# Top-8 expert selection in the router: eight rounds of maximum, index and knock-out in place of the MAX8 and FIND_INDEX8 instructions

## The reference

```python
router_logits = x @ gate_weight.T
router_probs = softmax(router_logits, axis=-1)                # 32 experts
router_top_value, router_indices = top_k(router_probs, 8)
routing_weights = router_top_value / clip(sum(router_top_value), 1e-12)
prim = router_indices[:, :4]; sec = router_indices[:, 4:]
sim_cand = sim[sec[:, :, None], prim[:, None, :]]
best_sim = max(sim_cand, -1); best_primary = prim at argmax(sim_cand, -1)
new_sec = where(best_sim < 0.5, sec, best_primary)
combine = sum(one_hot([prim, new_sec], 32) * routing_weights[..., None], 1)
for each expert e: y = y + (silu(x @ wg) * (x @ wu)) @ wd.T * combine[:, e]
```

## Time and profile before

| what | value |
|---|---|
| three timed runs | 7908.31, 8304.48 and 8369.88 us; median 8304.48 us |
| the profiled execution, whole | 7862.98 us |
| its span on the slowest core (core 0) | 7861.4 us |
| span of the other seven cores | 7813.4 to 7840.3 us |
| TensorE busy in matmuls | 5358.2 us, 68% of the span |
| VectorE busy | 2143.0 us, 27%, in 3227 instructions |
| ScalarE busy | 959.6 us, 12% |

### The profile page before, as it was taken

How to read it: one execution, slowest core, us unless ns; L and a number is a source line. 1 busy time by engine, 2 the same in 40 slices (tenths; PEclk the granted TensorE clock), 3 DMA queues, 4 the chain that set the end, 5 groups by cost and what they waited for, 6 DMA issues and landing times.

```text
span 7861.4 us, 58171 instructions; the slowest of 8 cores (7813.4 to 7861.4 us)
## 1 busy us (share of the span) xinstructions
PE 5358.2 (68%) x20631; PEld 2173.4 (28%) x21044; DVE 2143.0 (27%) x3227; ACT 959.6 (12%) x1288; POOL 34.6 (0%) x69
## 2 busy tenths in 40 slices
PE   3444665104777777777777787777777777777777
PEld 0111122001333333333333332333333333333332
DVE  5444544553222212121212121212122221212121
ACT  1103320000111010101010101010111101010101
POOL 0000000000000000000000000000000000000000
PEclk7766678556988888888888888888888888888888
DMA  4111001001332332333332323333323333333323
GB/s 163 38 48 59 1 23 58 9 0 58 101 103 98 106 98 104 97 108 99 106 100 104 96 103 97 104 101 102 103 100 100 100 104 99 105 94 106 100 107 123
DMA packets 146027, 692.91 MB, mean 88 GB/s; under 512 B 17136, under 2 KB 17264, under 8 KB 91696
## 3 DMA queue, kind: packets, MB, share of 16 engines
q1 hardware_dynamic: 136448, 646.94, 24.8%
q0 software_dynamic: 9296, 42.21, 1.6%
HBM read 680.70 MB, written 8.39 MB: 88 GB/s over the span
## 4 chain that ended last, share of the span: by engine, by line
PE 47%; DMA 21%; DVE 14%; issue 9%; ACT 8%; DVEq 1%; ACTq 0%; SPq 0%; POOL 0%; POOLq 0%
PE P L1162 37%; DMA arena_f<-wd 20%; ACT arena_b L1192 5%; DVE arena_b L1153 3%; DVE arena_f L1179 3%; PE P L1206 2%; PE P L678 2%; PE P L889 2%; PE P L828 1%; PE P L844 1%; ACT arena_b L783 1%; DVEq L158 1%; ACT arena_b L812 1%; PE P L507 1%; DMA arena_f<-wg 0%
## 5 line engine op out<-in xcount | busy, mean ns | idle before, releaser
L1162 PE MATMUL P<-arena_b 128*128 128x512 bf16 x12042 | 3042.9, 416 | 787.0 <-DVE arena_b L1153 767.9
L1162 PEld LDWEIGHTS P<-arena_b 128*128 128x128 bf16 x12288 | 1278.0, 105 | 2552.3 <-issue 1367.1
L1206 PE MATMUL P<-arena_b 128*128 128x512 bf16 x6020 | 1562.4, 419 | 583.5 <-ACT arena_b L1192 514.9
L1206 PEld LDWEIGHTS P<-arena_b 128*128 128x128 bf16 x6144 | 632.6, 106 | 1510.8 <-issue 965.4
L1214 DVE TENSOR_TENSOR arena_f<-arena_f,P 128x1024 f32<-128x1024 f32 x256 | 312.6, 1221 | 1808.1 <-PE P L1206 1808.1
L1153 DVE CAST arena_b<-arena_f 128x2048 bf16<-128x2048 f32 x384 | 469.7, 1223 | 1071.1 <-DMA arena_f<-wg 1071.1
L1179 DVE TENSOR_TENSOR arena_f<-arena_f,P 128x1024 f32<-128x1024 f32 x192 | 234.5, 1221 | 1857.2 <-PE P L1162 1857.2
L1192 ACT CAST arena_b<-arena_f 128x768 bf16<-128x768 f32 x512 | 425.5, 831 | 1704.9 <-DMA arena_f<-wd 1704.9
L1176 ACT ACTIVATE arena_f<-P 128x1024 f32<-128x1024 f32 x192 | 196.5, 1023 | 3372.5 <-PE P L1162 3353.2
L678 PE MATMUL P<-arena_b 128*128 128x512 bf16 x502 | 142.7, 450 | 196.4 <-DVE arena_b L671 195.6
L1182 DVE TENSOR_TENSOR arena_b<-arena_f 128x1024 bf16<-128x1024 f32 x192 | 235.3, 1225 | 20.0
(11 more groups left out here) (185 smaller groups left out, 1528.5 us busy)
## 6 DMA issues: line engine op xcount, KB each, us to landing
arena_f<-wg SPq DMA_DIRECT2D x384, 1024.0 KB, 4.9
arena_f<-wd SPq DMA_DIRECT2D x512, 384.0 KB, 3.1
arena_f<-x_win POOLq DMA_DIRECT2D x32, 768.0 KB, 5.1
arena_f<-wq SPq DMA_DIRECT2D x16, 1024.0 KB, 5.9
arena_f<-wo SPq DMA_DIRECT2D x16, 1024.0 KB, 6.0
arena_f<-x_win POOLq DMA_DIRECT2D x16, 512.0 KB, 14.5
out<-arena_f POOLq DMA_DIRECT2D x16, 512.0 KB, 3.5
arena_f<-wkv SPq DMA_DIRECT2D x4, 1024.0 KB, 5.5
```

What stands on the lines that cost most here:

```text
L1162: mk.op("pe", lambda E, ps=ps, par=par, c=c, s2=s2: E.matmul(out=ps[:, s2 * 512:(s2 + 1) * 512], lhsT=wbf2[par][:, c * 128:(c + 1) * 128], ...
L1206: first=(ei == 0 and j == 0): E.matmul(out=ps[:, s2 * 512:(s2 + 1) * 512], lhsT=wdbf[par][:, (ei * NDJ + j) * 128:(ei * NDJ + j + 1) * 128 ...
```

## The change

The three instructions of the top 8 (L1017, L1018, L1020) go, and with them the tensor `rIdx`. In their place VectorE copies the 32 probabilities to a scratch row and makes eight rounds. Round k takes the maximum of the row, compares the row with it, turns the comparison into 0 where it holds and 1,000,000 where not, adds the row 0..31, and takes the minimum, which is the first place of the maximum. The one-hot row `rH[k]`, which before was made after the weights, is now made in the round; in the first seven rounds three further operations set the chosen place of the scratch row to -1. The weights are computed after the rounds. `rws` has 320 columns in place of 512. Nothing else changes: not the other engines' instructions, not the DMAs, not the rest of the router, and the expert stage.

```diff
-        rI_t = st.enter_context(nc.sbuf_tensor("rIdx", [128, 8], U32))
...
-        r_ws, b_rws = A.alloc("rws", 64 * 8, F32, side="hi")
+        r_ws, b_rws = A.alloc("rws", 320, F32, side="hi")
...
-            mk.op("dve", lambda E: E.max(out=W0(8, 8), in_=W0(32, 32)), reads=[b_rws], writes=[b_rws])
-            mk.op("dve", lambda E: E.max_index(out=rI, in_max=W0(8, 8), in_values=W0(32, 32)),
-                  reads=[b_rws], writes=[b_rI])
-            mk.op("dve", lambda E: E.tensor_copy(out=W0(16, 8), in_=rI), reads=[b_rI], writes=[b_rws])
+            mk.op("dve", lambda E: E.tensor_copy(out=W0(224, 32), in_=W0(32, 32)),
+                  reads=[b_rws], writes=[b_rws])
+            for k in range(8):
+                mk.op("dve", lambda E, k=k: E.reduce_max(out=W0(8 + k, 1), in_=W0(224, 32), axis=AX.X),
+                      reads=[b_rws], writes=[b_rws])
+                mk.op("dve", lambda E, k=k: E.tensor_scalar(out=W0(256, 32), in0=W0(224, 32),
+                                                            scalar1=W0(8 + k, 1), scalar2=None,
+                                                            op0=ALU.is_equal),
+                      reads=[b_rws], writes=[b_rws])
+                mk.op("dve", lambda E: E.tensor_scalar(out=W0(288, 32), in0=W0(256, 32),
+                                                       scalar1=-1e6, scalar2=1e6,
+                                                       op0=ALU.mult, op1=ALU.add),
+                      reads=[b_rws], writes=[b_rws])
+                mk.op("dve", lambda E: E.tensor_tensor(out=W0(288, 32), in0=W0(288, 32),
+                                                       in1=iota_sb[:, 0:32], op=ALU.add),
+                      reads=[b_rws, b_iota], writes=[b_rws])
+                mk.op("dve", lambda E, k=k: E.tensor_reduce(out=W0(16 + k, 1), in_=W0(288, 32),
+                                                            axis=AX.X, op=ALU.min),
+                      reads=[b_rws], writes=[b_rws])
+                mk.op("dve", lambda E, k=k: E.tensor_single_scalar(
+                        out=rH[:, k * 32:(k + 1) * 32], in_=iota_sb[:, 0:32],
+                        scalar=W0(16 + k, 1), op=ALU.is_equal),
+                      reads=[b_rws, b_iota], writes=[b_rH])
+                if k < 7:
+                    mk.op("dve", lambda E, k=k: E.tensor_scalar(out=W0(256, 32),
+                                                                in0=rH[:, k * 32:(k + 1) * 32],
+                                                                scalar1=-1.0, scalar2=1.0,
+                                                                op0=ALU.mult, op1=ALU.add),
+                          reads=[b_rH], writes=[b_rws])
+                    mk.op("dve", lambda E: E.tensor_tensor(out=W0(224, 32), in0=W0(224, 32),
+                                                           in1=W0(256, 32), op=ALU.mult),
+                          reads=[b_rws], writes=[b_rws])
+                    mk.op("dve", lambda E, k=k: E.tensor_tensor(out=W0(224, 32), in0=W0(224, 32),
+                                                                in1=rH[:, k * 32:(k + 1) * 32],
+                                                                op=ALU.subtract),
+                          reads=[b_rws, b_rH], writes=[b_rws])
...
-            for k in range(8):
-                mk.op("dve", lambda E, k=k: E.tensor_single_scalar(
-                        out=rH[:, k * 32:(k + 1) * 32], in_=iota_sb[:, 0:32],
-                        scalar=W0(16 + k, 1), op=ALU.is_equal),
-                      reads=[b_rws, b_iota], writes=[b_rH])
```

More of the change, by code:

```diff
@@ L997, in build_nc @@
         cTb, b_cTb = A.alloc("cTb", 1024, BF16)
-        r_ws, b_rws = A.alloc("rws", 64 * 8, F32, side="hi")
+        r_ws, b_rws = A.alloc("rws", 320, F32, side="hi")
         rH, b_rH = A.alloc("rH", 8 * 32, F32, side="hi")
-        rI = rI_t[:, :]
-        b_rI = mk.buf("rI")
         for t in range(NQT):
```

## The result

The changed kernel is slower: its time over that of the kernel before is 1.0182, with a 95% interval of 1.0144 to 1.022, so about 143 us on 7863. The plain medians of ten runs each, 8013.65 us after (7983.27 to 8481.42) and 8017.3 us before (7849.05 to 8369.88), don't show it, since some executions in both sets (2 of 10 after, 5 of 10 before) ran longer with a lower TensorE clock on the cores of a die; the ratio leaves those out. The interval contains 1.02, so whether the slowdown reaches 2% is open. The profiled execution after took 8040.12 us, span 8038.5 us.

The account below looks back on a forecast made before the run. VectorE's chain in the router's tiles bounds the change: 18.49 us added less 0.94 is 17.55 per tile, 140.4 for eight, plus 1.3 late starts, 141.7 on 7862.98: 8005 us; likeliest 7980 to 8053, range's top 8512.

Parts of the forecast that it names:

- The chain: Router's eight tiles: each is one chain paced by VectorE, nothing hides added work; a tile goes from 57.0 to 74.6 us.
- work beside it: Rival, router tiles: the rounds lie beside other work, so 7863 us would stay; chance 0.01.
- cheaper operations: Rival, rounds in the router: each new operation takes only 0.16 us, total 7935 us, slower by 0.9%; chance 0.03.
- a starved VectorE: Rival, router tiles: VectorE gets instructions too slowly, 472 each 0.18 us late, 85 us more, 8090 us; chance 0.03.
- The removed search and the comparisons: Router tile: removing MAX8, FIND_INDEX8 and cast saves 0.94 us; eight one-hot comparisons only move, 2.78 us at unchanged cost.
- Operations with two constants: Rounds in the router: 15 per tile at 0.288 us from start to start, 4.32 us.
- The estimate of 7905 us beside the third rival: Router rounds: the skill's rule of 94 ns per two-tensor operation would give a total near 7905 us; no separate chance.
- The late starts: Router tiles: one VectorE instruction in 64 starts 0.18 us late, so 7 more among the 472 added, 1.3 us.
- The expert stage: Stage after the router: a later start changes it by 0, staying 6003 us within the cores' 48 us spread.
- the prediction's last sign: Expert stage: the prediction is wrong if this stage changes by more than 20 us.
- The rival that made of this a slowdown by the change: Expert stage: clock pattern falls worse on the slowest core, 24 us more, 8029 us, slower by 2.1%; chance 0.21.
- The call of no change: Whole kernel: forecast slowdown of 1.8% lies just below the 2% bound, so called no change; within 2% given 0.76.

Follow-up runs that it names:

- the repetition: The changed kernel run once more, unedited: 7987.42 us, expert stage's median 5968.8 us and its longest on a core 5983.5 us.
- the batched router: Kernel before with the router written for all eight tiles at once, only MAX8 and FIND_INDEX8 per tile: 7436.34 us; run again, ratio 0.9496.
- one placing: Kernel before plus 496 unused small VectorE instructions, two behind each of 248 gate and up weight conversions in the expert stage: 7884.78 us, repeated 7892.38 us.
- another: Kernel before plus the same 496 unused VectorE instructions, two by two behind the additions of the down projection: 7861.16 us.

## Why the prediction was right or wrong

*The chain.* Right. Nearly the whole price is one row, ScalarE's wait for the sum of the first four choices, 65.7 to 208.4 us. The three rivals that needed another place for it (work beside it, cheaper operations, a starved VectorE) are refuted: by the waits, by 2.74 us a round, and by the late starts below. One reading was short: VectorE does not wait for the others only in L1057, but also 5.9 us for the transpose at the end of a tile and 5.4 us for Exp. Both waits stayed (6.1 and 5.4 us after), so the sum did not suffer.

*The terms.* The removed search and the comparisons: as read. Two-tensor and reduction operations, 0.2925 us: 0.29 in the new rounds. Operations with two constants, taken from a single instruction at 181 ns (L465, which multiplies by one constant, so it was not quite the same form): 181 ns in both places where they stand, for 120 instructions; the bounds of 0.26 and 0.346 were not needed. The copy, which no row showed, is 181 ns too and 0.28 us from start to start. A tile's rounds from the trace after, 0.28 + 7 x 2.74 + 1.87 = 21.3 us with the moved comparisons, less 2.78 for those and 0.94 for the search, give 17.6 us (17.55 forecast). The estimate of 7905 us beside the third rival left out the gap between two instructions; with the ordinary 0.107 us, 62 x (0.094 + 0.107) - 0.94 = 11.5 us a tile, it would have been 7955 us. The 192 ns of a two-tensor operation decide against it either way.

*The late starts.* Mis-sized. I had 7 more of them and 1.3 us. The table of waits has 29 in 10.2 us in place of 21 in 6.0; above the ordinary gap of 0.107 us that is 7.1 against 3.8 us, so 3.3 us more. 8 x 17.6 + 3.3 = 144.1 us; measured over the cores' medians, 602.0 - 458.0 = 144.0, forecast 141.7.

*The expert stage.* Right that it does not change: 5967.6 to 5968.9 us in the median of the cores, and 5974.4 with the rounds twice. Also right that a single slowest core may be tens of microseconds off: 32 in one execution, and gone in the next. By the letter of the prediction's last sign (the stage changes by more than 20 us) those 32 us would have said that it was wrong; that sign lies within the spread of the cores, 48 us, and could not tell. The rival that made of this a slowdown by the change is refuted by the repetition.

*The call of no change.* Wrong, and this is the step that failed: "I call it no change by that bound, though every row says that the kernel does become slower". The sum gave 1.8% and the measured ratio is 1.0182, but the interval, 1.0144 to 1.022, lies wholly above 1. I had taken 2% as what a measurement can tell, for which no row stood; the measured interval reaches 0.4% to either side, from the 8 and 5 runs on which the ratio rests. A sum built from 472 instructions in a row, each with a price from a row, and without any cover, was a forecast of slower, and should have been called that, with the 2% line as a question of size. That the absolute 8005 us stands beside the median of 8013.65 us is partly luck. The sum was made for the profiled execution, which took 8040.12 us, and the ten runs of the kernel before alone have a median of 8017.3 us. The wide upper end of the range, which allowed for a set of runs like the first three, was not used.

## What to carry to other kernels

Count the instructions, not the data: on VectorE, as these traces show, a row of dependent operations on 32 columns costs about 0.29 to 0.35 us each, whatever they compute, and 8 columns cost 94% of that. Native multi-result operations (the search with its cast takes 0.94 us, the rounds in its place 18.6), fused two-step forms and wider tiles all pay by the count; the same instructions in a stage where VectorE waits for TensorE cost 10 to 33 us in place of 144. So ask first whether the stage has one chain, and if it has, read the price from start to start in the timeline and multiply; where many tiles go through such a chain one after another, put them side by side.

## What the runs showed of the hardware that was not expected

- A value per partition read from SBUF, in place of a constant, costs a VectorE operation about 60 ns: 241 ns for a comparison of 32 columns against 181 with constants, 231 against 172 at 8 columns, 252 against 193 in the two-step form. MAX8 (195 ns), FIND_INDEX8 (185 ns) and its load (92 ns) each cost no more than a plain operation on the same 32 columns. In the kernel before:

```profile
L1017 DVE MAX8 arena_f<-arena_f 128x8 f32<-128x32 f32 x8 | 1.6, 195 | 1.2 <-DVE arena_f L1014 0.5
...
L1018 DVE FIND_INDEX8 rIdx<-arena_f 128x8 uint32<-128x32 f32 x8 | 1.5, 185 | 0.0
...
L1018 DVE MATCH_VALUE_LOAD rIdx<-arena_f 128x8 f32 x8 | 0.7, 92 | 0.8
```

- A sum whose elements lie apart was slower. In the batched router the reduction of 2048 columns whose summed elements lie 32 apart took 3592 ns, where a two-tensor operation on 2048 took 2292; the reduction of 1024 neighbouring ones took 1222, as much as the two-tensor operation of that width (1225). The slow one also makes shorter sums, of 8 elements, but 32 sums of 4 neighbours each (L1058) took 286 ns against 293 for a two-tensor operation on as many columns, so shortness alone does not do it. It is one instruction, 3593 ns in the second run of this kernel:

```profile
L1052 DVE TENSOR_TENSOR arena_b<-arena_b 128x1024 f32<-128x1024 f32 x4 | 4.9, 1225 | 12.1 <-ACT arena_b L1041 11.8
L1055 DVE TENSOR_REDUCE arena_b<-arena_b 128x32 f32<-128x1024 f32 x4 | 4.9, 1222 | 0.4
L1082 DVE TENSOR_REDUCE arena_f<-arena_b 128x256 f32<-128x2048 f32 x1 | 3.6, 3592 | 0.1
...
L1081 DVE TENSOR_TENSOR arena_b<-arena_b 128x2048 f32<-128x2048 bf16 x1 | 2.3, 2292 | 0.1
...
L1059 DVE TENSOR_TENSOR arena_b<-arena_b 128x128 f32<-128x128 f32 x1 | 0.3, 293 | 0.1
L1058 DVE TENSOR_REDUCE arena_b<-arena_b 128x32 f32<-128x128 f32 x1 | 0.3, 286 | 0.1
```

- Small VectorE work beside TensorE can go with longer matmuls and no longer waits: 414 to 419 ns on core 1 in one placing, at a granted clock of 0.87 in place of 0.89, and 415 in another. The mechanism is open.
